# Rows of statistics and gates sent to all partitions by broadcast transfers from DRAM, in place of TensorE products of bf16 pieces

## Time and profile before

| | us |
|---|---|
| median of 3 runs (lowest, highest) | 2377.53 (2375.41, 2380.52) |
| the profiled execution | 2379.78 |
| its span, first to last instruction | 2377.8 |
| TensorE busy in the span | 2202.0 (93%) |
| VectorE | 1622.5 (68%) |
| ScalarE | 1222.9 (51%) |
| GpSimd | 918.5 (39%) |
| mean granted TensorE clock | 0.981 of full speed |

### The profile page before, as it was taken

One profiled execution on the slowest core, in us unless ns is written; L12 is line 12 of the kernel. 1 busy time (PEld: TensorE's weight loads), 2 busy tenths in 40 slices (PEclk: granted clock), 3 DMA queues, 4 the chain that ended last, 5 costly groups with the idle time before them and its releaser, 6 DMA issues. The chain is left out here.

```text
span 2377.8 us, 38759 instructions
## 1 busy us (share of the span) xinstructions
PE 2202.0 (93%) x9739; PEld 1071.6 (45%) x9739; DVE 1622.5 (68%) x4887; ACT 1222.9 (51%) x2030; POOL 918.5 (39%) x714
## 2 busy tenths in 40 slices
PE   6999999966999999999999999998999999999997
PEld 3555555533444444444444444444444444444443
DVE  6777777755677766767676666666667676767764
ACT  4444444434555555555555555555555555555553
POOL 1000000024455544445445555454544454554433
PEclk9999999987999999999999999999999999999998
DMA  3444444431122222222222222222222222222201
GB/s 146 163 162 162 162 162 162 162 122 46 62 73 73 74 81 76 81 85 75 73 73 73 73 73 72 73 73 73 81 82 91 73 73 73 73 73 84 73 33 59
DMA packets 66710, 216.99 MB, mean 91 GB/s; under 512 B 28496, under 2 KB 33328, under 8 KB 62640
## 3 DMA queue, kind: packets, MB, share of 16 engines
q1 hardware_dynamic: 66464, 215.71, 25.1%
q10 hardware_dynamic: 144, 0.30, 0.0%
HBM read 136.70 MB, written 77.47 MB: 90 GB/s over the span
## 5 line engine op out<-in xcount | busy, mean ns | idle before, releaser
L950 PE MATMUL ps<-hs,w_c 128*128 128x448 f32 x1792 | 806.9, 564 | 0.8 <-ACT yo L505 0.6
L495 ACT ACTIVATE hs<-ps,b1c,undo 128x448 f32<-128x448 f32 x896 | 602.6, 718 | 136.6 <-PE ps L941 136.0
L412 POOL TENSOR_TENSOR tl<-tr,th 128x448 f16<-128x448 f32 x224 | 245.5, 1096 | 515.7 <-ACT th L518 393.9
L854 PE MATMUL ps<-yo,cwT 128*128 128x448 bf16 x2016 | 425.6, 356 | 0.0
L950 PEld LDWEIGHTS ps<-hs,w_c 128*128 128x128 f32 x1792 | 305.3, 192 | 191.7 <-issue 152.3
L505 ACT ACTIVATE yo<-ps,cols 128x448 f32<-128x448 f32 x224 | 141.9, 633 | 453.6 <-PE ps L950 453.6
L407 POOL TENSOR_TENSOR xb<-xb,zr 128x448 f32<-128x448 f32 x224 | 259.1, 1159 | 182.7 <-ACT zr L511 181.8
L419 POOL TENSOR_TENSOR yo<-yo,base 128x448 f32<-128x448 f32 x224 | 264.5, 1181 | 167.4 <-DVE yo L781 166.6
L939 PE MATMUL ps<-th,w_h 128*128 128x448 f16 x896 | 321.4, 359 | 0.0
L941 PE MATMUL ps<-th,w_l 128*128 128x448 f16 x896 | 319.3, 356 | 0.0
L940 PE MATMUL ps<-tl,w_h 128*128 128x448 f16 x896 | 319.2, 356 | 0.0
(11 more groups left out here) (131 smaller groups left out, 2709.7 us busy)
## 6 DMA issues: line engine op xcount, KB each, us to landing
xb<-x SPq DMA_DIRECT2D x31, 1568.0 KB, 7.6
xb<-x SPq DMA_DIRECT2D x33, 896.0 KB, 4.7
result<-yo SPq DMA_DIRECT2D x32, 896.0 KB, 4.4
y_int<-y SPq DMA_DIRECT2D x32, 784.0 KB, 3.7
xb<-x SPq DMA_DIRECT2D x33, 672.0 KB, 4.3
result<-yo SPq DMA_DIRECT2D x32, 672.0 KB, 3.4
y<-y_int SPq DMA_DIRECT2D x32, 448.0 KB, 5.3
y<-y_int SPq DMA_DIRECT2D x32, 336.0 KB, 4.8
```

Source lines behind the costliest of these rows:

```text
L412: nc.gpsimd.tensor_tensor(cut(tl, c), tr[(b + c) % 2][:, :], cut(th, c), ALU.subtract).then_inc(tl_ready, 1)
L495: nc.scalar.activation(hs[(b + slot) % 2][:, j, :], ps[:, H_BANK + j, 0:T], ACT.Gelu_apprx_tanh, bias=b1c[:, j:j + 1], scale=undo[:, 1:2]) ...
L854: last = M(bank, cwT[:, t, :], sg[b][:, c * ROWS + dy:c * ROWS + dy + ROWS, dx:dx + SIDE], start=t == 0, stop=t == TAPS - 1)
L950: last = M(bank, w2_c[:, j, :], hs[(b + c) % 2][:, j, :], start=first, stop=final)
```

## The change

The three pieces go. `split_stats` only copies the rows from PSUM in float32, and `gates` ends with the gates in float32. SyncE writes them to DRAM: one transfer for the gates (`gate_row`), two for the statistics (`stat_rows`). From there ScalarE's queue sends them to all 128 partitions of three new tiles in SBUF (`gate_all`, and `stat_all` for 1/std and mean/std; 3136 float32 numbers a partition), each in two parts of 4 and 3 chunks: gates at step 17 of the turn after (`GATE_OUT_AT`), statistics at steps 27 and 29 (`STAT_OUT_AT`). VectorE reads its second operand from these tiles. `spread_stats` and `spread_gates` are gone, and with them 21 products an image; the banks BC0 and BC1 are left to the transposes. Some steps are later: the first scaling at 35 in place of 31, the first gating at 25 in place of 19.

```diff
-NORM_AT = [31, 39, 47, 54, 63, 71, 76]
-BASE_AT = [34, 42, 52, 58, 65, 73, 79]
+NORM_AT = [35, 41, 48, 55, 63, 71, 76]
+STAT_OUT_AT = [27, 29]
+BASE_AT = [38, 44, 52, 58, 65, 73, 79]
-OUT_AT = [19, 24, 29, 33, 38, 45, 52]
+OUT_AT = [25, 28, 31, 34, 38, 45, 52]
+GATE_OUT_AT = 17
...
+    g_dram = nc.dram_tensor("gate_row", [n_img, TOK], f32).ap()
+    s_dram = nc.dram_tensor("stat_rows", [2, n_img, TOK], f32).ap()
+        stat_all = [sb(f"stat_all{q}", [C, TOK], f32) for q in range(2)]
+        gate_all = sb("gate_all", [C, TOK], f32)
...
                     sp.wait_ge(gate_ready, n)
-                    for s in range(PIECES):
-                        sp.dma_start(rows[64 + s:65 + s, :].rearrange("a (r t) -> a r t", t=MR_COLS),
-                                     mks[:, s, :]).then_inc(gate_rows_in, 16)
+                    sp.dma_start(g_dram[bass.ds(n - 1, 1), :].rearrange("a (r t) -> (a r) t", t=MR_COLS),
+                                 mk[:, 5, :]).then_inc(gate_saved, 16)
                     sp.wait_ge(rms_ready, n + 2)
                     for q in range(2):
-                        for s in range(PIECES):
-                            sp.dma_start(rows[32 * q + s:32 * q + s + 1, :].rearrange("a (j p) -> a j p", p=TILE),
-                                         rms[:, s, q, :]).then_inc(norm_rows_in, 16)
+                        sp.dma_start(s_dram[q, bass.ds(n + 1, 1), :].rearrange("a (j p) -> (a j) p", p=TILE),
+                                     rms[:, q, :]).then_inc(stat_saved, 16)
...
+                    for m, mb, _ in due(GATE_OUT_AT, -1, n, b, pos):
+                        act.wait_ge(gate_saved, (m + 1) * 16)
+                        if has(m - 1):
+                            act.wait_ge(gated, m * NCH)
+                        for part in range(2):
+                            act.dma_start(gate_all[:, PART[part]], g_dram[bass.ds(m, 1), PART[part]]
+                                          .to_broadcast([C, (HALF, NCH - HALF)[part] * T])).then_inc(gate_in[part], 16)
+                    for m, mb, part in due(STAT_OUT_AT, 1, n, b, pos):
+                        act.wait_ge(stat_saved, (m + 1) * 32)
+                        for q in range(2):
+                            wait_count(act, (u_ready, t_ready)[q], (m - 1) * NCH + (HALF, NCH)[part])
+                            act.dma_start(stat_all[q][:, PART[part]], s_dram[q, bass.ds(m, 1), PART[part]]
+                                          .to_broadcast([C, (HALF, NCH - HALF)[part] * T])).then_inc(stat_in[q][part], 16)
...
-                link_stat(V.tensor_copy(rms[:, 0, :, :], src), m, 4)
-                link_stat(V.tensor_tensor(rrest[:, :, :], src, rms[:, 0, :, :], ALU.subtract), m, 5)
-                link_stat(V.tensor_copy(rms[:, 1, :, :], rrest[:, :, :]), m, 6)
-                V.tensor_tensor(rms[:, 2, :, :], rrest[:, :, :], rms[:, 1, :, :], ALU.subtract).then_inc(rms_ready, 1)
+                if has(m - 1):
+                    dve.wait_ge(stat_saved, m * 32)
+                V.tensor_copy(rms[:, :, :], src).then_inc(rms_ready, 1)
...
-                dve.wait_ge(bc_stats, 2 * g + 1)
-                V.tensor_tensor(ur[ring][:, :], cut(xb[b], c), ps[:, BC0, 0:T], ALU.mult).then_inc(u_ready, 1)
+                dve.wait_ge(stat_in[0][c // HALF], (m + 1) * 16)
+                V.tensor_tensor(ur[ring][:, :], cut(xb[b], c), cut(stat_all[0], c), ALU.mult).then_inc(u_ready, 1)
...
-                V.tensor_tensor(tr[ring][:, :], ur[ring][:, :], ps[:, BC1, 0:T], ALU.subtract).then_inc(t_ready, 1)
+                V.tensor_tensor(tr[ring][:, :], ur[ring][:, :], cut(stat_all[1], c), ALU.subtract).then_inc(t_ready, 1)
...
-                V.tensor_tensor(cut(yo[b], c), cut(yo[b], c), ps[:, BC1, 0:T], ALU.mult).then_inc(gated, 1)
+                V.tensor_tensor(cut(yo[b], c), cut(yo[b], c), cut(gate_all, c), ALU.mult).then_inc(gated, 1)
```

More of the change, by code:

```diff
@@ L37 @@
 EPS = 1e-5
-PIECES = 3
 T_SCALE = 1024.0
@@ L156, in block_kernel @@
         w1_f = base[1][:, 2 * C * TAPS:2 * C * TAPS + HID]
-        rows = sb("rows", [C, TOK], bf16)
         st = sb("st", [TILE, NT, 6], f32)
@@ L224, in block_kernel @@
         stat_rows = sem("stat_rows")
-        rms_h = sem("rms_h")
         rms_ready = sem("rms_ready")
-        norm_rows_in = sem("norm_rows_in")
-        bc_stats = sem("bc_stats")
+        stat_saved = sem("stat_saved")
+        stat_in = [[sem(f"stat_in{q}_{part}") for part in range(2)] for q in range(2)]
         u_ready = sem("u_ready")
@@ L247, in block_kernel @@
         gate_ready = sem("gate_ready")
-        gate_rows_in = sem("gate_rows_in")
-        bc_gate = sem("bc_gate")
+        gate_saved = sem("gate_saved")
+        gate_in = [sem(f"gate_in{part}") for part in range(2)]
         h_done = sem("h_done")
@@ L648, in tile_stats @@
                 last.then_inc(stats_taken, 1)
-            STAT_STEPS = 6
+            STAT_STEPS = 3
             mean2, dif, m2sum, sq, var_c, ve_c = (stw[:, i, :] for i in range(6))
@@ L689, in centre_tokens @@
                 ring = (b + c) % 2
-                dve.wait_ge(bc_stats, 2 * g + 2)
+                dve.wait_ge(stat_in[1][c // HALF], (m + 1) * 16)
                 dve.wait_ge(u_ready, g + 1)
@@ L770, in gates @@
                 link_mask(V.tensor_tensor(chosen, above, keep, ALU.add), n, 5)
-                link_mask(V.tensor_tensor(gate, chosen, wk[:, :], ALU.mult), n, 6)
-                link_mask(V.tensor_copy(mks[:, 0, :], gate), n, 7)
-                link_mask(V.tensor_tensor(grest[:, :], gate, mks[:, 0, :], ALU.subtract), n, 8)
-                link_mask(V.tensor_copy(mks[:, 1, :], grest[:, :]), n, 9)
-                V.tensor_tensor(mks[:, 2, :], grest[:, :], mks[:, 1, :], ALU.subtract).then_inc(gate_ready, 1)
+                if has(n - 1):
+                    dve.wait_ge(gate_saved, n * 16)
+                V.tensor_tensor(gate, chosen, wk[:, :], ALU.mult).then_inc(gate_ready, 1)
             def apply_gate(m, b, c):
                 g = m * NCH + c
-                dve.wait_ge(bc_gate, g + 1)
+                dve.wait_ge(gate_in[c // HALF], (m + 1) * 16)
                 dve.wait_ge(y_taken, g + 1)
-                V.tensor_tensor(cut(yo[b], c), cut(yo[b], c), ps[:, BC1, 0:T], ALU.mult).then_inc(gated, 1)
+                V.tensor_tensor(cut(yo[b], c), cut(yo[b], c), cut(gate_all, c), ALU.mult).then_inc(gated, 1)
             def phase2(n, b):
@@ L876, in transposes @@
                 pe.wait_ge(x1_ready, m * NCH + c + 1)
-                wait_count(pe, t_ready if c % 2 else u_ready, done(NORM_AT, 1, n, pos))
-                if c % 2:
-                    wait_count(pe, gated, done(OUT_AT, -1, n, pos))
+                if c % 2 == 0:
+                    wait_count(pe, rms_ready, done(STAT_AT, 1, n, pos))
                 if c > 1:
@@ L906, in rows_of_stats @@
                 last.then_inc(stat_rows, 1)
-            def spread_stats(m, b, c, n, pos):
-                g = m * NCH + c
-                if c == 0:
-                    pe.wait_ge(norm_rows_in, (m + 1) * 2 * PIECES * 16)
-                wait_count(pe, u_ready, g)
-                wait_count(pe, stats_taken, done(TRANSPOSE_AT, 1, n, pos + 1))
-                wait_count(pe, rms_ready, done(STAT_AT, 1, n, pos + 1))
-                M(ps[:, BC0, 0:T], ones_b[0:PIECES, :], cut(rows[0:PIECES, :], c), start=True, stop=True).then_inc(bc_stats, 1)
-                wait_count(pe, t_ready, g)
-                wait_count(pe, gated, done(OUT_AT, -1, n, pos + 1))
-                M(ps[:, BC1, 0:T], ones_b[32:32 + PIECES, :], cut(rows[32:32 + PIECES, :], c), start=True, stop=True).then_inc(bc_stats, 1)
-            def spread_gates(m, b, c, n, pos):
-                g = m * NCH + c
-                if c == 0:
-                    pe.wait_ge(gate_rows_in, (m + 1) * PIECES * 16)
-                wait_count(pe, gated, g)
-                wait_count(pe, t_ready, done(NORM_AT, 1, n, pos))
-                wait_count(pe, stats_taken, done(TRANSPOSE_AT, 1, n, pos + 1))
-                M(ps[:, BC1, 0:T], ones_b[64:64 + PIECES, :], cut(rows[64:64 + PIECES, :], c), start=True, stop=True).then_inc(bc_gate, 1)
             def hidden(n, b, c, j):
@@ L998, in phase2 @@
                         rows_of_stats(m, n, pos)
-                    for m, mb, c in due(OUT_AT, -1, *at):
-                        spread_gates(m, mb, c, n, pos)
-                    for m, mb, c in due(NORM_AT, 1, *at):
-                        spread_stats(m, mb, c, n, pos)
             pairs(pe, phase2, *P2, -1, n_img + 1)
```

11 lines of the change are left out of this document (3 added, 8 removed).

## The result

The changed kernel takes 2511.23 us (median of 4 runs, 2509.64 to 2512.62) against 2377.92 for the kernel before beside it: ratio 1.056, 95% interval 1.0542 to 1.0579. It is 133 us slower. The prediction, 2297.5 with a range of 2190 to 2410, has the wrong sign and its range misses the time. The profiled execution took 2509.6 (span 2507.7), 130 above that of before.

What follows compares the result with a forecast made beforehand. TensorE, busy 94% in the second phase, was taken as the bound. Per image 1.0 + 0.5 + 1.3 - 0.1 = 2.7 us, x 31 = 84, less 4 lost at the end: -80, so 2297.5 us, range 2190 to 2410.

Steps and rivals of the forecast that it cites:

- the term for wse in the first stretch: Before the search's first count: wse delayed 1.7 us by the statistics' broadcasts, leaving a gain of 1.0 us (0 to 2.7).
- Remove the wait at L917 alone and this one is late next: At the search's first count, L959: its 0.89 us wait is late next if only the wait for statistics rows goes.
- The spreads: On TensorE: 7 pairs and 7 single products an image removed, 5.6 us of 55.1.
- Collisions: VectorE's 21 operations now reading two SBUF tensors wait for GpSimd, 0.25 us each; 3.3 us an image in the search.
- The second rival: In the search, VectorE and GpSimd collide more than at random; at 0.56 us an operation, 2422 us; chance 0.20.
- third rival: Broadcasts slow or late: at half of 427 GB/s y lands late, TensorE waits some 8 us, 2540 us; chance 0.10.
- The page on queues: By turns between queues, wse delayed a packet or two only; first stretch gains near 2 us, some 30 us overall.
- what was to show it: First count waits some 1 us, following VectorE; operation means rise from 620 to some 800 ns; TensorE's busy share falls.

Runs made afterwards that it cites:

- quarter_bytes: Changed kernel with each broadcast of statistics written to 32 partitions in place of 128, the rest holding ones: 2377.3 us, ratio 0.9989 to the kernel before.
- stats_after_search: Changed kernel with statistics' broadcasts issued by SyncE behind wse and wk, first two scalings at steps 38 and 43: 2526.35 us, ratio 1.0651 to the kernel before.
- steps_only: Kernel before with the changed kernel's later step tables and nothing else, no broadcasts: 2448.93 us, ratio 1.0307.
- filled_wait: Changed kernel with 36 unused products of constants on TensorE before the first count of each search: 2473.88 us, ratio 1.0404 to the kernel before.
- one_input: Changed kernel with scaling, centring and gating reading one SBUF tensor and a column of ones, broadcasts transferred but unused: 2436.92 us, ratio 1.0255 to the kernel before.
- late_count: Changed kernel with the search begun 6 steps later and pressed together at its end, transfers unchanged: 2459.3 us, ratio 1.035 to the kernel before.

## Why the prediction was wrong

**The step that failed** is the term for wse in the first stretch, "I take 1.7, between them", with its bounds of 0 and 2.8. It let only the read of wse queue behind the broadcasts. The chain has two transfers behind one another, and both were delayed: w_row, 12 KB, by 5.15 - 1.44 = 3.7 us, wse by 5.58 - 3.41 = 2.2, together 5.9. The count ends at 2120.08, 12.25 us after L718 starts; before it was 8.94 us. For 2.7 us gained by SyncE, 5.9 were lost. quarter_bytes and stats_after_search show that it is the broadcasts that delay them. So the first stretch, forecast to gain 1.0 us with TensorE waiting some 1 us at the first count, has it waiting 7.08.

**The term that was missing** is TensorE's clock after a wait. steps_only and filled_wait show it. The profile of before had it too, more rarely: behind the wait at L917 the clock falls to half in 7 images, as here, 2 us after a wait of 1.29 us at 2229.29:

```profile
2229.00:2231.00 2.00, 1.68 (x8) 0.67 (x8) 1.22 (x2) 0.55 (x1) 0.00 (x0) 1.00 0.02 4
2231.00:2232.00 1.00, 0.88 (x3) 0.37 (x4) 0.50 (x2) 1.00 (x3) 0.12 (x1) 0.66 0.50 140
2232.00:2234.00 2.00, 2.00 (x7) 0.72 (x6) 1.10 (x4) 1.18 (x3) 2.00 (x2) 0.50 0.96 319
```

The mean of 0.99 over the phase hid these. With one wait of 2.2 to 2.8 us in their place it happens in most images, and with 6 to 9 us in all of them.

**The step tables** were costed at nothing of their own. "Remove the wait at L917 alone and this one is late next" named the mechanism; the sum then went on with a chain 2.7 us earlier, and did not ask what the later tables do if the chain is not. steps_only: +71.

**The spreads.** 5.6 us an image did go: TensorE's own work takes 2021 to 2026 us in filled_wait, where the clock is nearly as before, and 2202.0 - 5.6 x 32 is 2023. The two are estimates, good to some half us an image. This step was right.

**Collisions.** Means of 721, 795 and 812 ns against some 800 forecast, a rise of 0.16 us in the mean where 0.25 was taken: right in kind, the size a third lower. By one_input they cost 74 us at this place; GpSimd's own stretching, 1146 and 1176 ns in one_input against 1374 and 1427 for the additions, is in that and was not in the sum. The second rival's mechanism is real but is not what turned the sign. The Trainium skill, "SBUF — State Buffer", section "Who interferes with whom", has a VectorE instruction with two inputs in SBUF and a GpSimd instruction that reads SBUF block one another; the two groups of one_input agree.

**The rate of a broadcast** was feared to be half of a load's (third rival): it is not, 364 GB/s moved at a share of 0.99 while four of them run. y was not late in the kernel after (ScalarE's wait for it is 0.5 us, 109.6 before), since TensorE was later still; it was late again as soon as the search was less so (204.1 us in late_count).

**The page on queues.** By the Trainium skill, "DMA: Bandwidth & Descriptors", section "Queues, rings and completion order", each DMA engine takes turns between queues, a packet from each. The prediction worked out that wse would then be hardly delayed. The rows speak against using it so: with broadcasts on ScalarE's queue, 12 KB on SyncE's took 5.15 us. Why turns between queues still leave so small a transfer waiting, no run here shows. The same page, section "Latency and other measured facts", gives the latency of DRAM as 0.2 us in the mean and 2 us at high load; that would go in the direction of the 3.7 and 2.2 us, and no run here separates it from the queues.

Of what was to show it: L941 follows the counts and not ScalarE, but by 7 us and not 1; the means rose, two of three to some 800 ns; TensorE's share fell, far more than said.

Open are the clock's exact share (37 us at least, some 60 to 70 by the estimates), when a wait of 1 to 3 us brings the half clock and when not, what the transfers w_row and wse wait for beside the broadcasts, and why images alternate between 64.9 and 58.1 us (SyncE's L366 at 2040.78, 2105.64, 2163.76), which goes with the waits at L891.

## What to carry to other kernels

A bulk transfer added beside a chain of small dependent ones is paid at each link of the chain: list every transfer in flight at that time, find who waits for the last, and put the bulk where no such chain runs (the gates: a gain) or the chain's consumer later. When a wait is removed or a table moved, the idle time moves to the next late thing, and if it comes there in one piece TensorE can pay again in clock. And when a later table rescues a change, run the kernel before with the same table.

## What the runs showed of the hardware

- A 12 KB write to DRAM took 1.44 us to completion in the kernel before, 5.15 beside four broadcasts of another queue, and 1.38 (median) where these stood behind it; a 196 KB broadcast read took 3.41 us from issue to first use in the kernel before and 5.58 beside the broadcasts.
- After a wait of TensorE of 2.26 us the granted clock was 0.62 and then 0.50 for over 2 us (steps_only); of 30 waits of 2.2 to 2.8 us 22 were followed by the half clock and 8 not, and in the kernel before 7 of the images had it behind waits of some 1 us; after 7.08 us it was 0.50 until 5 us into the work that followed.
- A broadcast of one row to 128 partitions is about as quick as a plain load of the size: 896 KB of gates landed in 4.5 us in the median, and a load of 896 KB in 4.7. With four broadcasts in flight 896 KB of statistics took 6.0 us in the median, and 364 GB/s moved over the window, against 427 for the transfers of the earlier trace rows.
- GpSimd's additions stretched more (from 1.15 and 1.18 us to 1.37 and 1.43) than the VectorE operations that they met (from 0.62 to 0.72 to 0.81).
